# Four early value products, the stacks' first copy ahead of the routing's exponential, and maxima over experts 4 to 7

## The reference

```
xn = layernorm(x)
x = x + favor_attention(xn) + local_transformer(xn)    # first layer
xn2 = layernorm(x)
x = x + attention(xn2) + mixture_of_experts(xn2)       # second layer
```

## Time and profile before

| | |
|---|---|
| median of 3 runs | 2047.99 us |
| profiled execution | 2054.12 us |
| its span | 2052.3 us |
| PE busy | 1831.4 us, 89% |
| VectorE (DVE) busy | 1322.1 us, 64% |
| ScalarE (ACT) busy | 761.4 us, 37% |
| GpSimd (POOL) busy | 274.9 us, 13% |
| mean granted clock of TensorE | 0.95 |

### The profile page before, as it was taken

How to read it: one execution, slowest core, us unless ns; L and a number is a source line. 1 busy time by engine, 2 the same in 40 slices (tenths; PEclk the granted TensorE clock), 3 DMA queues, 4 the chain that set the end, 5 groups by cost and what they waited for, 6 DMA issues and landing times.

```text
span 2052.3 us, 43524 instructions
## 1 busy us (share of the span) xinstructions
PE 1831.4 (89%) x18228; PEld 1064.9 (52%) x18228; DVE 1322.1 (64%) x2768; ACT 761.4 (37%) x1442; POOL 274.9 (13%) x222
## 2 busy tenths in 40 slices
PE   6988989889898898988989889898898898988898
PEld 3655546555455544555445544556555464554644
DVE  5776557755677556775577754777547874468744
ACT  3224252343432434324433244332453333533234
POOL 2020110211101101111021010220102201022010
PEclk9999999999999999999999989999999998999989
DMA  5001100010000200002000020000200002000020
GB/s 190 8 1 19 15 6 7 2 25 9 7 7 2 31 2 6 7 2 31 2 7 7 2 32 2 12 1 3 31 3 12 1 2 31 2 7 1 3 31 8
DMA packets 27765, 29.79 MB, mean 15 GB/s; under 512 B 3684, under 2 KB 26004, under 8 KB 27156
## 3 DMA queue, kind: packets, MB, share of 16 engines
q1 hardware_dynamic: 27572, 27.01, 6.9%
HBM read 12.06 MB, written 2.36 MB: 7 GB/s over the span
## 4 chain that ended last, share of the span: by engine, by line
PE 62%; DVE 19%; ACT 8%; DMA 4%; issue 4%; SPq 3%; ACTq 0%; DVEq 0%
PE bank L986 6%; PE bank L776 5%; PE bank L1001 5%; PE bank L1011 4%; DMA phi<-parts 4%; PE bank L718 3%; PE bank L808 3%; DVE ls L1578 3%; SPq L464 3%; PE bank L866 2%; PE bank L1024 2%; ACT phi L1341 2%; ACT phi L1201 2%; ACT lc L1341 2%; PE bank L658 2%
## 5 line engine op out<-in xcount | busy, mean ns | idle before, releaser
L1743 DVE TENSOR_REDUCE amx<-bank 128x2 f32<-128x512 f32 x256 | 162.0, 685 | 77.5 <-PE bank L1024 77.5
L1307 ACT ACTIVATE silu<-bank 128x512 f32<-128x512 f32 x144 | 84.5, 596 | 290.3 <-PE bank L986 277.9
L1731 DVE TENSOR_TENSOR mh<-bank,silu 128x512 f32<-128x512 f32 x144 | 99.6, 692 | 133.7 <-PE bank L1001 131.1
L1578 DVE RECIPROCAL ls<-bank 128x256 f32<-128x256 f32 x64 | 112.2, 1753 | 61.8 <-PE bank L828 61.7
L986 PE MATMUL bank<-xn2T,w_mw 128*128 128x512 f32 x288 | 151.0, 645 | 0.0
L1011 PEld LDWEIGHTS bank<-w_mw,mh 128*128 128x128 f32 x1152 | 137.1, 192 | 25.5 <-issue 25.5
L1011 PE MATMUL bank<-w_mw,mh 128*128 128x128 f32 x1152 | 143.4, 278 | 0.0
L516 POOL TENSOR_TENSOR xB<-xn2T,lsq 128x512 f32<-128x512 f32 x32 | 40.8, 1274 | 765.1 <-ACT lsq L1313 765.1
L497 POOL TENSOR_TENSOR lc<-lc,ls 128x512 f32<-128x512 f32 x32 | 40.8, 1276 | 631.1 <-DVE lc L1531 631.1
L718 PE MATMUL bank<-hT,w_wqkv 128*128 128x512 f32 x256 | 119.1, 603 | 5.8 <-ACT hT L1281 5.7
L1563 DVE TENSOR_REDUCE lmx<-bank 128x4 f32<-128x512 f32 x128 | 79.5, 684 | 56.9 <-PE bank L776 56.9
(11 more groups left out here) (295 smaller groups left out, 3698.6 us busy)
## 6 DMA issues: line engine op xcount, KB each, us to landing
phi<-parts SPq DMA_DIRECT2D x96, 64.0 KB
lc<-parts SPq DMA_DIRECT2D x96, 64.0 KB
w_mw<-in_mw SPq DMA_DIRECT2D x3, 1152.0 KB
x_in<-in_x SPq DMA_DIRECT2D x8, 256.0 KB, 2.8
out<-res SPq DMA_DIRECT2D x8, 256.0 KB, 2.3
w_wqkv<-in_wqkv SPq DMA_DIRECT2D x2, 768.0 KB, 6.4
w_w<-in_w SPq DMA_DIRECT2D x1, 682.0 KB, 4.2
mh<-in_rotary SPq DMA_DIRECT2D x1, 512.0 KB, 6.0
```

The source lines that it names most:

```text
L1307: A(silu[:, n % 2, :], bank_of("moe_g", n)[:], ACT.Silu).then_inc(sem["moe_silu"], 1)
L1578: V.reciprocal(lrec[:, k % 2, :], bank_of("loc_den", k)[:, 0:SEQ]).then_inc(sem["loc_rec"], 1)
L1731: V.tensor_tensor(mh[:, n % 4, :], bank_of("moe_u", n)[:], silu[:, n % 2, :], ALU.mult).then_inc(sem["moe_h"], 1)
L1743: V.tensor_reduce(amx[:, 2 * b:2 * b + 2, h], bank_of("att_max", n)[:].rearrange("p (t k) -> p t k", t=2), AX.X, ALU.max).then_inc(sem["at ...
```

## The change

Three things change. EARLY is 4: all four values of the next turn stand between L948 and L555 on PE, and their four copies in front of the xn2T copy on ScalarE; value 2 behind the attention values and value 3 of layer 0 are gone. On ScalarE the copy of part 1 stands ahead of the router's exponential. And no maxima stand in expert 3; experts 4 to 7 have four pairs each: one behind the gate, one behind the unit, two behind the output. Banks follow: PLACE puts the router into bank 1 and query and key into banks 0 and 2, xn2T goes to bank 7, and most jobs of layer 0 and of the experts move on by one bank in their ring.

```
-        EARLY = 3
+        EARLY = 4
-        MAX_AT = {3: ((), (), (0, 1)), 4: ((2,), (3,), (4, 5)), 5: ((6,), (7,), (8,)),
-                  6: ((9,), (10,), (11, 12)), 7: ((13,), (14,), (15,))}
+        MAX_AT = {q: ((4 * q - 16,), (4 * q - 15,), (4 * q - 14, 4 * q - 13)) for q in range(4, EX)}
...
+                   "att_nmT": "seven", "favor_qk": "seven", "favor_v": "spare", "xn2T": "spare", "att_v": "acc", "att_sT": "five", "loc_pv": "norm", "loc_nmT": "rows", "favor_out": "norm"}
+        PLACE = {("route", 0): 1, ("att_qk", 0): 0, ("att_qk", 1): 2,
...
                     last.then_inc(sem["loc_sum_ps"], 1)
-                    values(3)
+                    if l:
+                        values(3)
...
                 if it + 1 < TURNS:
-                    for j in range(2):
+                    for j in range(EARLY):
                         early_value(it + 1, j)
...
-                if it + 1 < TURNS:
-                    early_value(it + 1, 2)
...
                 if it + 1 < TURNS:
-                    early_value(it + 1, 0)
+                    for j in range(EARLY):
+                        early_value(it + 1, j)
                 act.wait_ge(sem["xn2T_ps"], now("xn2T_ps", 1))
                 A(xn2T[:], bank_of("xn2T")[:], ACT.Copy).then_inc(sem["xn2T"], 1)
...
-                if it + 1 < TURNS:
-                    early_value(it + 1, 1)
...
-                act.wait_ge(sem["route_d"], now("route_d", 1))
-                A(rsm[:, 4:6, :], rsm[:, 2:4, :], ACT.Exp).then_inc(sem["route_exp"], 1)
                 act.wait_ge(sem["att_qk"], now("att_qk", 2))
                 act.wait_ge(sem["stack_in"], prior("stack_in"))
                 A(parts[:, :, 0, :], aqk, ACT.Copy).then_inc(sem["att_part1"], 1)
+                act.wait_ge(sem["route_d"], now("route_d", 1))
+                A(rsm[:, 4:6, :], rsm[:, 2:4, :], ACT.Exp).then_inc(sem["route_exp"], 1)
...
                 gates(0)
-                if it + 1 < TURNS:
-                    early_value(it + 1, 2)
```

More of the change, by code:

```diff
@@ L261, in build @@
         ORDER = [EX] + list(range(EX))
-        MAX_AT = {3: ((), (), (0, 1)), 4: ((2,), (3,), (4, 5)), 5: ((6,), (7,), (8,)),
-                  6: ((9,), (10,), (11, 12)), 7: ((13,), (14,), (15,))}
+        MAX_AT = {q: ((4 * q - 16,), (4 * q - 15,), (4 * q - 14, 4 * q - 13)) for q in range(4, EX)}
         RINGS = {"short": range(0, 6), "long": range(6, 8), "quad": range(0, 4), "norm": range(4, 8), "rows": [3, 7, 3, 6], "wide": [4, 5, 6, 0], "wide1": [4, 5, 7, 0],
-                 "five": range(0, 5), "seven": [0, 1, 2, 3, 4, 7, 5], "acc": [6], "tail": [7, 5], "spare": [7], "late": [5]}
+                 "five": range(0, 5), "seven": [0, 1, 2, 3, 4, 7, 5], "acc": [6], "tail": [7, 5], "spare": [7]}
         RING_OF = {"favor_pv": "long", "att_pv": "tail", "loc_ss": "long",
@@ L269, in build @@
                    "route_T": "seven", "moe_g": "seven", "moe_w": "seven", "moe_u": "seven", "att_max": "seven",
-                   "att_nmT": "seven", "favor_qk": "seven", "favor_v": "spare", "att_v": "acc", "att_sT": "five", "loc_pv": "norm", "loc_nmT": "rows", "favor_out": "norm"}
-        PLACE = {("loc_rb", 1): 6, ("loc_rb", 2): 4, ("loc_rb", 3): 5, ("loc_rb", 5): 4, ("loc_rb", 6): 5, ("loc_rb", 7): 7,
+                   "att_nmT": "seven", "favor_qk": "seven", "favor_v": "spare", "xn2T": "spare", "att_v": "acc", "att_sT": "five", "loc_pv": "norm", "loc_nmT": "rows", "favor_out": "norm"}
+        PLACE = {("route", 0): 1, ("att_qk", 0): 0, ("att_qk", 1): 2,
+                 ("loc_rb", 1): 6, ("loc_rb", 2): 4, ("loc_rb", 3): 5, ("loc_rb", 5): 4, ("loc_rb", 6): 5, ("loc_rb", 7): 7,
                  ("favor_score", 12): 0, ("favor_score", 13): 4, ("favor_score", 14): 5, ("favor_score", 15): 6,
@@ L279, in job @@
         def job(name, k, freed_by, count, ahead=0):
-            ring = "late" if (name, k, ahead) == ("loc_v", 2, 1) else ("quad", "wide", "quad", "wide1")[k // 4] if name == "loc_max" else "long" if (name, k) in LONG else RING_OF[name] if name in RING_OF else "short"
+            ring = ("quad", "wide", "quad", "wide1")[k // 4] if name == "loc_max" else "long" if (name, k) in LONG else RING_OF[name] if name in RING_OF else "short"
             i = PLACE[name, k] if (name, k) in PLACE else RINGS[ring][turns_of[ring] % len(RINGS[ring])]
@@ L314, in build @@
             job("loc_sum", l, "loc_sum", l + 1)
-            job("loc_v", TT * l + TT - 1, "loc_v", TT * l + TT)
+            if l:
+                job("loc_v", TT * l + TT - 1, "loc_v", TT * l + TT)
             favor_jobs(l, "sums")
@@ L369, in build @@
         job("att_v", 0, "att_v", 1)
-        job("loc_v", 2, "loc_v", 3, ahead=1)
         def weight_job(q):
```

## The result

The kernel after takes 2000.01 us (median of 4 runs, 1998.07 to 2000.82) against 2047.7 for the kernel before (4 runs of it beside them, 2046.06 to 2054.14). The ratio is 0.9754, 95% interval 0.9732 to 0.9776. The profiled execution took 2000.41 (span 1998.6) against 2054.12: 53.7 us less where the sum said 36.3. Of the difference of 17.4, 6 come from the profiled execution of before, which was 6.4 above its median; between the medians 47.7 were won. The forecast was too small, and the number nearest to the result is rival D's (2004).

What follows compares the result with a forecast made beforehand. TensorE, at 89% of the span, was taken to bound the kernel. Edits 32.8, clock after the DMA wait 9.7, layer 0 -6.2: 36.3 us off 2054.1 gives 2017.8, weighed against 2011.7 from the median to 2016; range 2000 to 2037.

Steps and rivals of the forecast that it cites:

- rival D: Slow stretches at the router and behind the DMA wait go, layer 0 stays as is: 2004 us, chance 0.11.
- Early values: Norm wait before L555: four values cut idle to 13 us, clock holds in seven turns, first gate 3.8 us earlier.
- Rival A: Clock still falls before the routing, so the copy starts only 0.1 us earlier: 2036 us, chance 0.14.
- Copy: ScalarE at the routing: part 1 copied ahead of the exponential, so the DMAs of the stacks start 2.84 us earlier.
- the FIFO rule: ScalarE is strict FIFO, so the exponential waits behind the copy: 0.9 us of last-turn routing, hidden, sum unchanged.
- Maxima: Wait at L1024: gate(4) runs first, 1.91 us won per turn; at the end 0.2 lost, 1.2 in the last turn.
- I keep 24.1: The 24 DMAs still take 24.1 us from first issue to last landing, as no gap opens in their queue.
- The clock after the DMA wait: First maximum to expert 4's output product: of 15.2 us clock loss a third, 5.5, remains; 9.7 gained.
- The clock in layer 0: L738 to L776: without value 3 the clock falls in all 8 turns, 1.5 us each; 6.2 us lost.
- The psum-queue rule: Short idles between groups of matmuls can make the clock go up and down; applied to the 6.2 us layer 0 loss.
- B: The clock's fall in layer 0 is long in all turns, 26 us instead of 6: 2036 us, chance 0.10.
- C: Slower: half clock from layer 0's root lasts into local attention's maxima and scores; 2060 at 15 us per turn, chance 0.05.

Runs made afterwards that it cites:

- copy alone: The kernel before with only the copy of part 1 put ahead of the exponential: 2041.1 us, ratio 0.9963.
- The repetition: The kernel after, unchanged, profiled a second time: one execution, 2002.74 us.
- swap: The kernel after with the banks of loc_rb 5 and loc_rb 6 exchanged: 1999.1 us, ratio 0.9755 to the kernel before.

## Why the prediction was too small

**Early values: right, bar two turns.** Idle before L555 13.9, forecast 13. Clock 1.00 in five of seven turns, forecast seven. The filler ahead of the norm wait and value 3 put back show that the work in this wait decides: with 2.2 us of idle a turn the clock fell in every turn, with 1.3 in few. Rival A did not occur.

**Copy: right in mechanism, 0.2 us too good in size.** The copy starts at 4.95 (forecast 4.8), the DMAs 2.64 earlier instead of 2.84, and 1.7 in the two turns with a fall. The exponential waits for VectorE (L1703), not for the copy. Where it does wait for the copy (copy alone) it is 1.03 late and PE waits for nothing: the FIFO rule of the Trainium skill that the prediction cites ("Perfetto Trace Analysis", section "Tensor Engine Instruction") holds and costs PE nothing, as the sum had it.

**Maxima: right in mechanism; the DMAs' length was not.** Gate(4) is done meanwhile, and L1066 waits 2.2 us in all (forecast 7 x 0.2 + 1.2 = 2.6). The first two terms with it, 32.8 forecast, came to 36.6: from the first transpose to the start of the attention the eight turns take 51.8 less, of which 15.2 are clock behind the wait. The starts of the DMAs are 17.7 earlier in the seven turns, forecast 7 x 2.84 = 19.9, so 2.2 are missing. The step that failed is "I keep 24.1" for the 24 DMAs, a term put at nothing: their lengths sum to 195.5 instead of 201.3, 5.8 less, 4.8 of it in turns 7 and 8 (23.6 and 23.3 instead of 26.1 and 25.6). The repetition has it too (194.0), and the experiments show that it goes with the copy ahead of the exponential. With it the term closes: 17.7 + 5.8 + 8 x 1.91 - 2.2 = 36.6. It is also why the wait came to 10.8 where about 15 was forecast.

**The clock after the DMA wait: mis-sized.** "I take a third of it to remain, 5.5" against 0: 15.2 were gained instead of 9.7. The profiled execution flatters here: the repetition kept 3.2, and of the three kernels nearest to it the exchange kept 4.9, the filler in layer 0 3.2 and the filler in the last turn 0. The experiments bear out the direction, that the clock falls in more turns as the waits grow: 8 of 8 at 36.4 and 39.9 us of wait in all, 4 to 6 of 8 at 17.8 to 23.6, 0 to 3 of 8 at 12.5 and below. 

**The clock in layer 0: wrong in number and in price.** "Without it I expect the fall in all 8 turns" did not come true: it fell in 4, and in 6 in the repetition. But the price per fall was not 1.5: from L738 to L777 the four cost 8.2, and the stretch behind, up to the output product, another 1.8, so 2.5 each. Before, the same two stretches had 5.8 and 0.2. The loss is 4.0, forecast 6.2. That value 3 was "the only dense work in it" is not so. Behind the root, ahead of L776, stand four products of 128 by 128 by 512, here in the second turn of the kernel before:

```profile
307.21 1.04 PE L764 MATMUL bank<-w_winmask,w_ident 128*128 128x512 bf16 x4
```

Nor does value 3 decide alone: with one dense product put back in its place the clock fell in 6 of 8. That taking it out costs something was right (3 to 4 us on the mean of the kernels). The psum-queue rule of the Trainium skill that the prediction weighed ("TensorE: Matmul & The Clock Gate", section "A second HAM failure mode: psum-queue depth-cycling") is half borne out: short idles did go with a changing clock, but not turn by turn.

**The rest of the layers: not in the prediction.** By the new bank order the fifth loc_rb waits for a bank that VectorE's L1498 still holds (0.32 us, swap); L738 to L777 of layer 1 went from 10.04 to 10.47, 3.3 us over the kernel, and the stretch from there to the next transposes gave 3.6 back (433.7 to 430.1). That agrees with swap, whose total shows no gain. Outside these: the first turn reaches L738 1.7 earlier (PE's wait for the first constant's DMA was 7.5 instead of 9.0; it was 7.3 to 8.1 in all the other kernels), the stretch from layer 0's output product to L738 of layer 1 is 2.0 shorter (1.6 of it in the last turn, which has no slow stretch there), the last attention 0.9 and the end 0.9, and 0.1 lies between the turns. No edit is aimed at these 5.6, and I have not traced them further. Layers and ends: -4.0 - 3.3 + 3.6 + 5.6 = 1.9 gained, forecast 6.2 lost.

Against the forecast, the three terms are 36.6, 15.2 and 1.9 for 32.8, 9.7 and -6.2: 3.8 + 5.5 + 8.1 = 17.4 off, all on one side. No single step carries it. Three parts are of one size: the length of the DMAs, kept at 24.1 each (5.8), the third of the clock loss kept behind the wait (5.5), and the 5.6 that no term was made for. Layer 0 (2.2) comes next, and the starts of the DMAs (2.2) go the other way. Of these the DMAs' length is the surest, since the repetition has it in full, and 3.2 of the 5.5 came back there. Rival D, "both slow stretches go and layer 0 stays as it is", is near by its number and in part by luck. Behind the DMA wait the slow stretch did go, at the router it remained in two turns, half as long, and layer 0 did not stay but lost 4.0; the DMAs and the unassigned 5.6 made up for it. Rivals B and C did not occur.

What stays open: why a clock fell in one turn and not in another with the same wait, why fillers in the layers went with the router's falls, and why the DMAs of the last two turns are shorter with the copy ahead.

## What to carry to other kernels

A stall on TensorE can cost more behind itself than in itself, so read the granted clock of the stretch behind each wait and price the two together; a product moved into the wait, even a useless one, can pay more than its own time. An edit that makes one engine early is worth nothing while another queue's order (here an exponential in front of a copy) keeps the transfer from starting: time the edits in pairs before dropping one. Judge a slow stretch by when PE reaches the next places, and go on to the end of the stage: in layer 1 it costs next to nothing up to the scores and 2.3 us up to the transposes behind the maxima. And look at the stages behind a filler too, since what it wins in one can be lost in the next.

## What was not expected of the hardware

- The same wait and the same work before and behind it bring the clock down or not: 3.30 us with none, 3.32 us with 3.4 us at half. In the kernel with the two banks exchanged it fell in one turn after 1.55 us. The Trainium skill says of starts that the number of slow matmuls is "run-variable" ("TensorE: Matmul & The Clock Gate", section "Part 1: The HAM clock gate (the "warmup" mystery)"); that holds here for falls in the middle of a kernel too.
- 24 equal DMAs of 64 KB took from 22.4 to 26.7 us from first issue to the first maximum, wherever PE waits for them. The length hangs on the turn: 25.9 to 26.7 in the first and third, 22.4 to 23.2 in the sixth, in every kernel. In the seventh it hangs on the kernel: 24.1 to 26.1 with the exponential ahead of the copy, 23.1 to 23.4 with the copy ahead.
- Dense work ahead of layer 1's scores went with a router that, some 60 us later, lost its clock in 4 or 5 turns of 7 (three kernels) instead of 0 to 2 (the ten others with the same idle).
